# The last expert mixture's gate: the bias row added by TensorE, the top values read straight from PSUM

## What is computed

```python
def _L1_ffn_ref(x, Wg, bg, We, be):
    probs = jax.nn.softmax(x @ Wg + bg, axis=-1)        # 256 logits for each token
    idx = jnp.argmax(probs, axis=-1)
    p = jnp.take_along_axis(probs, idx[..., None], axis=-1)[..., 0]
    e_idx = idx % We.shape[0]                            # one of 8 experts
    h = jax.nn.relu(jnp.einsum('bsd,edf->besf', x, We) + be[None, :, None, :])
    onehot = jax.nn.one_hot(e_idx, We.shape[0], dtype=x.dtype)
    return jnp.einsum('besf,bse->bsf', h, onehot) * p[..., None]
...
x = x + _L1_ffn_ref(_layernorm(x, axis=-1), ...)         # the end of the reference
```

## Time and profile before

| | us |
|---|---|
| three timed runs | 1171.85, 1180.72, 1183.11 |
| their median | 1180.72 |
| the profiled execution's own time | 1175.31 |
| its span, from the first to the last instruction | 1173.5 |
| TensorE busy | 1046.4 (89%) |
| VectorE busy | 726.5 (62%) |
| ScalarE busy | 614.3 (52%) |
| GpSimd busy | 221.8 (19%) |
| mean granted TensorE clock | 0.934 of full speed |

### The profile page before, as it was taken

One profiled execution on the slowest core, in us unless ns is written; L12 is line 12 of the kernel. 1 busy time (PEld: TensorE's weight loads), 2 busy tenths in 40 slices (PEclk: granted clock), 3 DMA queues, 4 the chain that ended last, 5 costly groups with the idle time before them and its releaser, 6 DMA issues. The chain is left out here.

```text
span 1173.5 us, 18594 instructions
## 1 busy us (share of the span) xinstructions
PE 1046.4 (89%) x6202; PEld 570.2 (49%) x6202; DVE 726.5 (62%) x1804; ACT 614.3 (52%) x1305; POOL 221.8 (19%) x360
## 2 busy tenths in 40 slices
PE   7989999999899899999967999996989999998380
PEld 4532333333364334444466999994533444446360
DVE  4767787877478798889370000005679988856632
ACT  2236666666622587777713444431337877784250
POOL 2000000000110214153302222211001111021255
PEclk9969999999999799999967999998979999999695
DMA  9954433330049332421286855625964332302164
GB/s 301 322 151 115 110 92 74 91 74 2 2 186 312 69 82 57 100 69 35 88 343 224 318 184 177 187 70 175 324 181 109 80 90 67 69 15 72 27 180 143
DMA packets 76878, 157.51 MB, mean 134 GB/s; under 512 B 9261, under 2 KB 26289, under 8 KB 75377
## 3 DMA queue, kind: packets, MB, share of 16 engines
q1 hardware_dynamic: 72704, 146.09, 41.6%
q0 software_dynamic: 4080, 10.23, 3.3%
HBM read 102.03 MB, written 52.17 MB: 131 GB/s over the span
## 5 line engine op out<-in xcount | busy, mean ns | idle before, releaser
L960 ACT ACTIVATE r<-ps 128x512 f32<-128x512 f32 x768 | 418.0, 600 | 189.1 <-PE ps L1074 188.4
L411 DVE TENSOR_REDUCE m<-ps 128x1 f32<-128x512 f32 x512 | 321.0, 683 | 49.0 <-PE ps L1043 49.0
L1074 PE MATMUL ps<-stacks 50*128 50x512 f32 x768 | 286.0, 463 | 8.3 <-DMA stacks<-mT 5.0
L1043 PE MATMUL ps<-stacks 48*128 48x512 f32 x720 | 288.1, 477 | 3.7 <-DVE r L488 3.0
L1074 PEld LDWEIGHTS ps<-stacks 50*128 50x128 f32 x768 | 122.0, 191 | 183.6 <-ACT r L960 125.7
L1083 PE MATMUL ps<-r 128*32 128x512 f32 x1536 | 209.8, 619 | 1.6 <-ACT r L960 1.6
L407 DVE CUSTOM_DVE_ANT_0 r<-ps,r 128x512 bf16<-128x512 f32 x256 | 166.0, 688 | 54.0 <-PE ps L1043 53.3
L1731 DVE TENSOR_TENSOR r<-ps,r 128x256 f32<-128x256 f32 x46 | 19.5, 425 | 194.6 <-PE ps L1779 167.6
L1043 PEld LDWEIGHTS ps<-stacks 48*128 48x128 f32 x720 | 117.7, 193 | 24.4 <-DVE m L411 14.6
L886 POOL CAST mparts<-m 128x16 fp32r<-128x16 f32 x48 | 9.8, 205 | 554.1 <-DVE m L411 318.6
L1695 ACT ACTIVATE r<-ps,b1c 128x128 f32<-128x128 f32 x184 | 52.5, 368 | 94.0 <-PE ps L1761 94.0
(11 more groups left out here) (149 smaller groups left out, 1034.9 us busy)
## 6 DMA issues: line engine op xcount, KB each, us to landing
r<-in_w SPq DMA_DIRECT2D x31, 1024.0 KB, 6.0
stacks<-q_parts SPq DMA_DIRECT2D x96, 192.0 KB, 3.6
stacks<-k_parts SPq DMA_DIRECT2D x96, 192.0 KB, 4.5
k_parts<-r SPq DMA_DIRECT2D x24, 512.0 KB, 3.6
q_parts<-r SPq DMA_DIRECT2D x24, 512.0 KB, 4.3
k_parts<-r SPq DMA_DIRECT2D x24, 256.0 KB, 4.2
q_parts<-r SPq DMA_DIRECT2D x24, 256.0 KB, 3.7
r<-in_ctxT SPq DMA_DIRECT2D x8, 512.0 KB, 5.1
```

The costliest lines, as they stand in the source:

```text
L411: ins = dve.tensor_reduce(out, mem.ps[:, bank, :], AX.X, ALU.max)
L960: act.activation(mem.probs[:, u // HG, u % HG, :], ps[:, ST + unit_of(b, g, u) % DEEP, :], ACT.Exp, scale=SCALE).then_inc(a.p_exp.sem, 1)
L1043: pe.matmul(ps[:, led_bank(n), :], stack_of(mem.qst[g], h, ROWS)[:, t * P:(t + 1) * P], stack_of(mem.kst[g], h, ROWS), start=True, stop=Tr ...
L1074: pe.matmul(ps[:, ST + N % DEEP, :], stack_of(mem.kst[g], h, KROWS)[:, kt * P:(kt + 1) * P], stack_of(mem.qst[g], h, KROWS), start=not a.m ...
```

## The change

In the last mixture only (`m.hidden is None`; the first mixture's gate runs the same instructions as before):

- The bias row is no longer added by VectorE. For each tile TensorE first multiplies a row of ones (`mem.one`, one partition of 128 ones, set once by GpSimd) by the bias row (one partition, 256 columns, float32) with `start=True`, and the two products with the weights add to it.
- `max`, `max_index` and ScalarE's exponentials read the logits in PSUM. The SBUF copy is not written.
- The logits of even batches lie in banks 2 and 3, those of odd batches in banks 4 and 5. TensorE waits from batch 2 on: for the searches and the exponentials of the batch two before.
- There are two buffers for the exponentials and two for `ntop` (placed in a tile of the finished attention). VectorE's wait for the exponentials stands before `ntop` from batch 2 on, not before the additions.
- ScalarE starts the exponentials of a pair of tiles when VectorE has searched that pair, since both read the same bank.

```diff
 def gate_vector(dve, m):
     def body(b):
-        if m.hidden is None:
-            dve.wait_ge(m.exps.sem, m.exps.at(b))
-        for k in range(2):
-            ...
-            dve.tensor_tensor(mem.logits[:, 2 * k:2 * k + 2, 0:m.width], got, row, ALU.add).then_inc(m.logit.sem, 1)
+        if m.hidden is not None:
+            for k in range(2):
+                sums_of(b, k)
         for t in range(T):
-            dve.wait_ge(m.logit.sem, m.logit.at(b, t // 2 + 1))
-            dve.max(mem.top8[:, t, :], mem.logits[:, t, 0:m.width]).then_inc(m.choice.sem, 1)
+            if m.hidden is not None:
+                dve.wait_ge(m.logit.sem, m.logit.at(b, t // 2 + 1))
+            elif t % 2 == 0:
+                dve.wait_ge(m.g_ps.sem, m.g_ps.at(b, t // 2 + 1))
+            dve.max(mem.top8[:, t, :], logits_of(b, t)).then_inc(m.choice.sem, 1)
         if m.hidden is None:
             dve.wait_ge(m.choice.sem, m.choice.at(b, T))
-            dve.tensor_scalar(mem.ntop[:, :], mem.top8[:, :, 0], -1.0, None, ALU.mult).then_inc(m.ntop.sem, 1)
+            if b >= 2:
+                dve.wait_ge(m.exps.sem, m.exps.at(b - 1))
+            dve.tensor_scalar(mem.ntop[b % 2], mem.top8[:, :, 0], -1.0, None, ALU.mult).then_inc(m.ntop.sem, 1)
         for t in range(T):
             dve.wait_ge(m.choice.sem, m.choice.at(b, t + 1))
-            dve.max_index(mem.idx8[:, t, :], mem.top8[:, t, :], mem.logits[:, t, 0:m.width]).then_inc(m.choice.sem, 1)
+            dve.max_index(mem.idx8[:, t, :], mem.top8[:, t, :], logits_of(b, t)).then_inc(m.choice.sem, 1)
 def gate_gpsimd(pool, m):
+    if m.hidden is None:
+        pool.memset(mem.one, 1.0).then_inc(m.one_ready.sem, 1)
 def gate_scalar(act, m):
             for t in range(T):
-                act.activation(mem.exps[:, t, :], mem.logits[:, t, :], ACT.Exp, bias=mem.ntop[:, t:t + 1],
+                if t % 2 == 0:
+                    act.wait_ge(m.choice.sem, m.choice.at(b, T + t + 2))
+                act.activation(mem.exps[b % 2][:, t, :], logits_in(m, b, t), ACT.Exp, bias=mem.ntop[b % 2][:, t:t + 1],
                                accum_out=mem.sum[:, b, t:t + 1]).then_inc(m.exps.sem, 1)
 def gate_tensor(pe, m):
     def body(b):
-        pe.wait_ge(m.logit.sem, m.logit.at(b))
+        if m.hidden is not None:
+            pe.wait_ge(m.logit.sem, m.logit.at(b))
+        elif b >= 2:
+            pe.wait_ge(m.choice.sem, m.choice.at(b - 2, 2 * T))
+            pe.wait_ge(m.exps.sem, m.exps.at(b - 1))
+        banks = LOGITS[b % 2 if m.hidden is None else 0]
         for k in range(2):
             for t in range(2):
+                out = ps[:, banks[k], t * m.width:(t + 1) * m.width]
+                if m.hidden is None:
+                    pe.matmul(out, mem.one, mem.rows[0:1, m.row, :], start=True, stop=False)
                 for c in range(C):
-                    ins = pe.matmul(ps[:, 2 + k, t * m.width:(t + 1) * m.width],
-                                    mem.rnT[b % 2][:, c, (2 * k + t) * P:(2 * k + t + 1) * P], mem.gate[:, c, 0:m.width],
-                                    start=(c == 0), stop=(c == C - 1))
+                    ins = pe.matmul(out, mem.rnT[b % 2][:, c, (2 * k + t) * P:(2 * k + t + 1) * P],
+                                    mem.gate[:, c, 0:m.width], start=(c == 0 and m.hidden is not None), stop=(c == C - 1))
             ins.then_inc(m.g_ps.sem, 1)
     def rest_of_batches():
+        if m.hidden is None:
+            pe.wait_ge(m.one_ready.sem, 1)
```

More of the change, by code:

```diff
@@ L107, in __init__ @@
         self.m = sb("m", [P, 2, SIDES, PAIRS * T])
+        self.ntop = [self.m[:, i, 0, 0:T] for i in range(2)]
         self.mparts = sb("mparts", [P, P])
@@ L123, in __init__ @@
         self.expert_u = sb("expert_u", [P, T], U32)
-        self.ntop = sb("ntop", [P, T])
         self.sum = sb("sum", [P, B, T])
@@ L192, in __init__ @@
         self.be = take(self.r1, E * D, [E, D])
+        self.one = take(self.r1, P, [P])[0:1, :]
         at[0] = 0
@@ L225, in __init__ @@
         at[0] = 0
-        self.exps = take(self.r2, T * D, [T, D])
+        self.exps = [take(self.r2, T * D, [T, D]) for _ in range(2)]
         at[0] = gate_from
@@ L1314, in __init__ @@
             self.ntop = sig("ntop", 1)
+            self.one_ready = sig("one_ready", 1)
             self.exps = sig("exps", T, T)
@@ L1345, in __init__, with logits_in @@
             self.out_stored = Signal(out_stored, 16)
+LOGITS = (2, 3), (4, 5)
+def logits_in(m, b, t):
+    return m.mem.ps[:, LOGITS[b % 2][t // 2], t % 2 * m.width:(t % 2 + 1) * m.width]
 def gate_vector(dve, m):
@@ L1367, in normalise, with sums_of @@
         ins.then_inc(m.rn_ready.sem, 1)
-    def body(b):
-        if m.hidden is None:
-            dve.wait_ge(m.exps.sem, m.exps.at(b))
-        for k in range(2):
-            dve.wait_ge(m.g_ps.sem, m.g_ps.at(b, k + 1))
-            got = ps[:, 2 + k, 0:2 * m.width].rearrange("p (t d) -> p t d", t=2)
-            row = mem.rows[:, m.row:m.row + 1, 0:m.width].to_broadcast([P, 2, m.width])
-            dve.tensor_tensor(mem.logits[:, 2 * k:2 * k + 2, 0:m.width], got, row, ALU.add).then_inc(m.logit.sem, 1)
-        for t in range(T):
-            dve.wait_ge(m.logit.sem, m.logit.at(b, t // 2 + 1))
-            dve.max(mem.top8[:, t, :], mem.logits[:, t, 0:m.width]).then_inc(m.choice.sem, 1)
+    def sums_of(b, k):
+        dve.wait_ge(m.g_ps.sem, m.g_ps.at(b, k + 1))
+        got = ps[:, LOGITS[0][k], 0:2 * m.width].rearrange("p (t d) -> p t d", t=2)
+        row = mem.rows[:, m.row:m.row + 1, 0:m.width].to_broadcast([P, 2, m.width])
+        dve.tensor_tensor(mem.logits[:, 2 * k:2 * k + 2, 0:m.width], got, row, ALU.add).then_inc(m.logit.sem, 1)
@@ new lines, in logits_of @@
+    def logits_of(b, t):
+        if m.hidden is None:
+            return logits_in(m, b, t)
+        return mem.logits[:, t, 0:m.width]
+    def body(b):
+        if m.hidden is not None:
+            for k in range(2):
+                sums_of(b, k)
+        for t in range(T):
+            if m.hidden is not None:
[3 more added lines that the diff above has]
+            dve.max(mem.top8[:, t, :], logits_of(b, t)).then_inc(m.choice.sem, 1)
```

## The result

The changed kernel takes 1189.15 us (median of 13 runs, 1184.86 to 1194.48), the kernel before 1181.54 us (13 runs, 1171.85 to 1192.28). The ratio is 1.0078, 95% interval 1.0050 to 1.0105: slower by 0.8%. Forecast were 1186 us and 8.3 us more (0.7%), so the change is a small loss, as forecast. The profiled execution took 1186.05 us, its span is 1184.2.

What follows compares the result with a forecast made beforehand. VectorE bounded the gate; with 16 tiles at 1.69 us TensorE would, putting `onehot` 8.3 us later. 1175.31 + 8.3 = 1183.6 us, put on the middle of four times (1178.0): 1186 us, 8-in-10 range 1176 to 1195.

Steps and rivals of the forecast that it cites:

- The bound: Last mixture's gate: VectorE bounds it, busy 19.75 of 20.5 us; with the change TensorE becomes the bound.
- The deciding term: TensorE's gate products: a one-row bias call 0.43 us, each change-of-shape block 0.20 extra; a tile 1.69 us instead of 0.86.
- rival A: Gate products: no cost for the change of shape, a tile 1.29 us, `onehot` +2.0 us, 1180 us in all; chance 0.20.
- The sum of the gate: From first product to `onehot`: TensorE's queue ends at 1099.98, then two `max` and the rest; `onehot` at 1102.92, 8.3 us later.
- Reading PSUM: `max`, searches and exponentials reading logits from PSUM cost nothing extra; the skill's table would give 65 ns for each on VectorE.
- The covers: Behind `onehot`: batch 3's exponentials end about 0.3 us after the reciprocal's turn, covered by 0.8 us of waiting for counting products.
- the gain of up to 0.5 us from the faster clock: Counting products after the gate: TensorE's shorter idleness may let them run faster, worth up to 0.5 us, left to the range.
- The tail: From `onehot` to the end: the distance stays as before, so the gate's loss passes to the whole, microsecond for microsecond.
- The whole: Whole kernel: 1186 us, with 8.3 us more than before; within 1% of no change, chance 0.78.
- Rival C: TensorE's clock falls within the gate, from batch 1 on 15.6 us more: +24 us, 1202 us in all; chance 0.07.
- Rival B: Gate products: the bias call costs next to nothing, `onehot` 4.3 us earlier, 1174 us in all; chance 0.05.

Runs made afterwards that it cites:

- experiment 6: Kernel before, with only the logits of odd batches moved to banks 4 and 5; gate 23.8 us, ratio to the kernel before 0.9998.
- experiment 3: Changed kernel without the bias calls, so the bias is left out of the logits; gate 20.1 us, ratio to the kernel before 0.9942.
- full_rows: Changed kernel with the ones held in 128 rows (one of ones, 127 of zeros); gate 25.7 us, ratio to the kernel before 0.9980.
- no_bias: Changed kernel without the bias calls, the same run as experiment 3; gate 20.1 us, ratio to the kernel before 0.9942.
- bank_row: Changed kernel with one bias call of 512 columns for a bank instead of two of 256; gate 28.7 us, ratio to the kernel before 1.0028.
- after_again: Changed kernel with nothing edited, run again on chip 1; gate 31.8 us, ratio to the kernel before 1.0030.
- after_third: Changed kernel with nothing edited, run a third time, on chip 3; gate 31.8 us, ratio to the kernel before 1.0090.
- rows64: Changed kernel with the ones held in 64 rows (one of ones, 63 of zeros); gate 31.8 us, no ratio given.
- rows96: Changed kernel with the ones held in 96 rows (one of ones, 95 of zeros); gate 25.8 us, no ratio given.
- parts_full: Changed kernel with the bias split into three bf16 rows, added by one 128-row bf16 call for a bank; gate 20.8 us, ratio to the kernel before 0.9987.
- parts_full_2: The kernel with the bias as three bf16 rows, unchanged, run again on chip 3; gate 20.9 us, ratio to the kernel before 0.9974.
- banks_only: Kernel before, with only odd batches' logits moved to banks 4 and 5, the same run as experiment 6; gate 23.8 us, ratio 0.9998.
- experiments 2, 4, 8, 12: Changed kernel with ones in 128 rows, one bias call for a bank, ones in 64 rows, ones in 96 rows; gates 25.7, 28.7, 31.8, 25.8 us.

## Why the prediction was right

**The bound.** That VectorE bounded the gate was right: removing TensorE's wait alone gave nothing (experiment 6), and taking the additions away without putting anything in their place gave 3.7 us (experiment 3).

**The deciding term.** 0.43 us of stream for a bias call and 0.20 us for each block between two changes of shape: 1.69 us for a tile against 1.69 measured. The comparison by which the prediction took 0.43 us for one row was loose, since the 50-row rows have 512 columns and the gate's 256; full_rows (0.44 us with 128 rows) and 0.63 - 0.20 = 0.43 with one row show it like for like. Both halves are shown apart. Against no_bias the gate grows by 5.6 us with the stream alone (full_rows), and by another 6.1 with the narrow operand, for 32 blocks 0.19 each; halving the blocks takes away 3.2 (bank_row). Without the second half the change would have come out at +2.0 us, as rival A says (full_rows: 25.7 - 23.8 = +1.9). Reading the 0.20 off four rows of the attention, was what made the forecast. What the runs show is the price and the loads that no longer run ahead; what the array does in that time, they do not show.

**The sum of the gate.** Forecast 1102.92 - 1070.82 = 32.10 us, measured 31.83. The rest is small terms. The transposes after batches 0 and 1 have the array's whole shape too, so the weights' block in front of them has no change behind it: 1075.38 - 1074.41 = 0.97 us, not 1.06. The very last block, with its run-out, takes 1.13 us and not 1.06 + 0.24. A round of transposes takes 0.97 us and not 0.94. Together TensorE's stretch was forecast 0.4 us too long (29.16 against 28.78). From its end over two `max` to `ntop` it is 0.84 us and not 0.75, and from `ntop` to `onehot` 2.21, not 2.19.

**Reading PSUM.** `max` takes 424 ns where it took 412 from SBUF, the search 422 where it took 419; it is 12 and 3 ns more. The cycle table of the Trainium skill (VectorE: DVE Perf Modes, section on the TRN2 errata), from which the prediction estimated 65 ns more each, differs from that, and the measurement decides. ScalarE's exponentials went from 496 to 473 ns, with 203 instead of 186 for reading the sum.

**The covers.** The forecast had the late exponentials hidden behind the counting products: they need 0.3 us of a cover of 0.8. In the first profile after, TensorE's granted clock is 1.00 (2.4 GHz) in its 3.4 us of idleness and in these products; before it was 0.50 (1.2 GHz) in them, after 5.0 us of idleness. They are through early (`under` 1.16 us after `onehot`, before it was 1096.19 - 1094.59 = 1.60). So the reciprocal, which waits 0.37 us for ScalarE, ended 0.02 us ahead of `under`, and the chain of waits runs through the exponentials:

```profile
1098.51 0.82 DVE idx L1407 x2
...
1099.41 0.77 ACT r L1481 x3
...
1100.25 1.10 ACT r L1481 x5
...
1101.45 0.25 DVE prob L1576
```

The cover was used up, and the gain of up to 0.5 us from the faster clock came to 0.44. In after_again and after_third, after the same 3.4 us of idleness, the granted clock in these products is 0.50 and `under` comes 1.61 us after `onehot`. So the clock there is one or the other from one execution to the next. Neither touches the result.

**The tail.** "The distance from `onehot` to the end as before" was wrong for the first profile by 4.7 us, and right within 1.1 us for after_third and for the rows64 and rows96 kernels (77.8 to 79.1). A single profile on each side would have put 12.8 us, from the gate's first product to the end, on the change.

**The whole.** The median of the kernel before was 1181.54 us in 13 runs and not the 1178.0 on which the sum was put; the difference, 7.6 us by the medians and 9.2 by the ratio, holds the 8.3 forecast. Rival C did not occur: the clock stays at 1.00 through the gate. Rival B's condition, a bias that costs less than 0.31 us for a tile, is what parts_full makes true with 0.11, by another kind of call; its gate gives back 2.9 us of the 4.3.

**Why the ratios scatter.** On chip 1 all four ratios lie below what the gates of the traces give: after_again +3.5 us for +8.05, full_rows -2.4 for +1.9, no_bias -6.8 for -3.7, bank_row +3.3 for +4.9. On chips 2 and 3 parts_full has -1.5 for -2.9, after_third +10.6 for +8.05 and parts_full_2 -3.0 for -2.9. The granted clock accounts for it. Each timed run has its mean granted clock, from 0.926 to 0.943, and among the runs of one kernel on one chip a run is 9.2 us faster for each 0.01 that it is higher, with a scatter of 1.2 us about that line (174 runs fitted with one slope). On chip 1 the runs of the kernel before happened to have 0.934 in the mean and those of after_again and full_rows 0.939. At equal clock (0.936) the differences from the kernel before are these:

| | at equal clock, us (95%) | by the gate, us |
|---|---|---|
| after_again (1) | +8.4 (0.9 either way) | +8.05 |
| full_rows (1) | +2.4 (0.9) | +1.9 |
| no_bias (1) | -3.9 (0.9) | -3.7 |
| bank_row (1) | +5.5 (0.9) | +4.9 |
| banks_only (2) | -0.1 (0.9) | 0.0 |
| parts_full (2) | -3.0 (0.9) | -2.9 |
| after_third (3) | +8.7 (0.9) | +8.05 |
| parts_full_2 (3) | -2.4 (0.9) | -2.9 |

So the whole time follows the gate in all eight, and parts_full is faster than the kernel before by a difference clear of the scatter. At the same clock the kernel before takes 1179.3 us on chip 1, 1174.6 on chip 2 and 1174.5 on chip 3; the changed kernel takes 1187.7 on chip 1, 1183.2 on chip 3 and 1187.9 in its first runs, whose profile has the standstill too. The runs of the kernel before beside those first ones come without their clocks, so the +7.6 us of the first comparison can't be put right in this way. The traces show that this time is lost or won ahead of the gate: the gate begins at 1068.73 us in the first profile of the changed kernel (clock 0.941), at 1065.98 in after_again (0.940) and at 1075.18 in after_third (0.933).

## What to carry to other kernels

Moving an addition from VectorE to TensorE is paid at the price of a matmul of the same columns, and if the operand is narrow, at the price of two changes of shape as well: pad it with zero rows to the shape of its neighbours, or put one call where there were two. Here padding took away 6.1 of the 8.1 us and was still a small loss; only the cheaper call made a gain of it. Before an operation is moved off the busiest engine, add up the engine that receives it: here it stood idle for 7.5 us of the 20.5 and was given 13.3. A float32 row can be added in one bf16 pass if it is split into three bf16 rows. And before a difference of a few microseconds is read from whole times, compare runs at equal granted clock, or read the stretch that was changed in the trace.

## What the runs showed of the hardware

- Between float32 calls with a 128-row operand, a block of calls with 1 or 64 rows costs 0.19 to 0.20 us extra, and so does a 128-row block between two such; one that has such a neighbour only ahead of it costs 0.11 (0.97 against 0.86). 96 rows cost nothing extra (experiments 2, 4, 8, 12). At a change the first weight load starts with its product, otherwise 0.22 us before it.
- A one-row call takes the time of its columns, 0.63 - 0.20 = 0.43 us for 256 float32 columns, as one with 128 rows (0.44).
- One bf16 call of 512 columns between float32 calls takes 0.21 us, where the float32 bias of the same two tiles took 0.87 in full shape.
- On one of three chips, in all four profiles taken there, the engines stand still at the same place, until about 25 us after `onehot` (TensorE 2.7 to 3.7 us, GpSimd 1.9 to 2.0), and the tail is some 5 us longer; in eight profiles on the two others they run through it, the changed kernel's among them.
- Runs of these kernels differ in their mean granted clock (0.926 to 0.943), and 0.01 of it goes with 9.2 us of these 1180.
